# Order of the late expert teams, and the place of the first row fetch, in a routed-expert kernel on one core

## The chip, the core and the metric

The kernel runs on one core of a Trainium2 chip. The metric is the device time of one execution in microseconds (us). The core has a matrix engine (TensorE, "PE" in the profile), a vector engine (VectorE, "DVE"), a scalar engine (ScalarE, "ACT"), GpSimd ("POOL"), and SyncE ("SP"), which here only issues transfers. Sixteen DMA engines move data for all of them. An engine runs its own instructions in their order and waits on semaphores that the others raise.

## The reference

One block of three sublayers works on 256 tokens of width 512: cross-attention to 4096 memory rows under a mask, causal self-attention with 16 heads, and a layer of 64 experts of which each token takes 8. Only the last sublayer is touched:

```python
router_logits = x @ gate_w                                   # 256 x 64
routing_weights, selected = jax.lax.top_k(router_logits, K)  # K = 8
routing_weights = jax.nn.softmax(routing_weights, axis=-1)
hidden_sorted = jnp.repeat(x, K, axis=0)[order]              # rows sorted by expert
gate = jax.lax.ragged_dot(hidden_sorted, gate_proj_w, group_sizes)   # 512 -> 192 for each expert
up = jax.lax.ragged_dot(hidden_sorted, up_proj_w, group_sizes)
down = jax.lax.ragged_dot(jax.nn.silu(gate) * up, down_proj_w, group_sizes)
out = jnp.sum(down[unsort].reshape(-1, K, h) * routing_weights[..., None], axis=1)
```

The input x of this layer is layer-normed, and the result is added to the residual. An expert has 1152 KB of weights (gate 384, up 384, down 384), so the 64 experts have 72 MB, and each of them is read once whatever the routing is.

## The kernel before

**Teams and rounds.** The experts are worked off in 16 teams of four (`TEAM = 4`). TensorE takes a team in rounds of 32 rows for each of its four experts (`BLK = 32`), 128 rows in all, one quarter of the array's columns for each expert. So a team costs as many rounds as its largest expert has blocks of 32 rows, while its weights cost 4.5 MB of transfer however few rows it has.

**Order of the teams.** Teams 0, 1 and 2 (`EARLY = 3`) are experts 0 to 11 as numbered, so that their weights can be loaded before the routing is known. The other 52 experts are sorted by size on the chip (L819 to L822, `place` is the rank, largest first). The row `turn_row` says which rank stands at each position of the order: two iotas (L527 to L529) fill the pairs of teams, from `FIXED` upwards (the largest) and from `EXP_N - TEAM` downwards (the smallest), in turns, and a last one sets the middle team at the end. Counting the rows that the reference's router gives each expert for these inputs (0 to 138), the rounds of teams 0 to 15 are

```
3, 1, 1 | 5, 1, 3, 1, 3, 1, 2, 1, 2, 1, 1, 1, 1      28 rounds, numbered 0 to 27 below
```

**The ring.** Weights stand in a ring of four slots (`RING = 4`); team q uses slot q mod 4. SP issues 16 transfers for a team: gate and up of four experts (`load_gate_up`, L396), then down in two parts each (`load_down`, L403). Teams 0 to 2 are loaded during attention; team 3 once the list of teams is there (L417 to L418). From team 4 on (`reload`) SP first waits until TensorE has done the gate and up products (`s_gu`) of all rounds of the teams up to q - 4, issues the gate and up loads, waits for the same rounds' down products (`s_y`), and issues the down loads. `team_of` unpacks four expert numbers from one word into registers ahead of all issues (L385).

**A round on TensorE** (`one_round`, L1324): 32 gate and up products (L1329, `s_gu`); the mix of the last round's outputs into the tokens (L1251); products that turn the picks and give the weight of each slot (L1350, L1353, `s_mtp`); the turn of the hidden values (L1359); the turn of the next round's gathered rows (L1365), which waits until ACT has copied them (L1019); a product that gives the row numbers of the round three on (L1293); and 24 down products (L1378, `s_y`). Round 0 is written apart (`first=True`): rows for rounds 0 and 1 come from products with pick matrices (L1276), not from a gather, and before L1350 it waits for `s_wp` (weight parts, from POOL) and `s_tn`.

**Rows by gather.** From round 2 on POOL fetches a round's 128 rows (256 KB) of x from memory: `fetch(u, b)` is one small operation (L567) and an indirect transfer (L568) by the row numbers `row_no`, which DVE writes (L858, `s_idx`). In the loop POOL fetches round u, then waits for the landing of the fetch before it and says so (L625, `s_land`), and then forms rank differences for a later pick (L591, `differences`). ACT's copy L1019 waits for `s_land`. Ahead of the loop POOL does `differences(2)` and `differences(3)`, then four operations that split the router weights in three parts (L604 to L607, the last raises `s_wp`), then reads the number of rounds, then waits for the parts and the stored rows of x (`s_xp`, `s_xd`) and for `s_idx`, and issues the first fetch, `fetch(2, 0)`.

**Engines in a round.** DVE turns the slot weights from L1353 into `w_slot` (L884, L886); ACT scales the expert output with it (L1024); DVE finishes it (L890); the next round's L1251 takes both.

Of the kernel before, what the change touches and what calls it, by code (L numbers as in the profile page):

```python
# [19 lines left out]
P = 128  # L20
TOK, D = 256, 512
TH = TOK // P
# [7 lines left out]
EXP_N, TOPK, INTER = 64, 8, 192  # L30
TEAM = 4
# [5 lines left out]
FIXED = EARLY * TEAM  # L37
# [14 lines left out]
def perceiver(nc, x, ctxm, mask, w_qkv, w_out, q_gain, gate_w, gate_proj, up_proj, down_proj,  # L52
              rope_cs, out):
    es = ExitStack()
    with es:
# [7 lines left out]
        bank = [psum[:, i, :] for i in range(8)]  # L63
# [303 lines left out]
        def _(sp):  # L367
# [15 lines left out]
            def team_of(word):  # L383
                for j in range(TEAM):
                    sp.reg_mov(lanes[j], (word >> (6 * j)) & (EXP_N - 1))  # L385
                return [sp.snap(lanes[j], min_val=0, max_val=EXP_N - 1) for j in range(TEAM)]

            def word_of(q):
                return sp.value_load(team_word[0:1, bass.ds(q, 1)], min_val=0, max_val=EXP_N ** TEAM - 1)

            def load_gate_up(team, r):
                for j, e in enumerate(team):
                    lane = ring[r][:, j]
                    for dst, src in ((lane[:, 0:GU_W], gate_proj[bass.ds(e, 1)].rearrange("e (p c) n -> p (e c n)", c=DC)),
                                     (lane[:, GU_W:DOWN_AT], up_proj[bass.ds(e, 1)].rearrange("e (p c) n -> p (e c n)", c=DC))):
                        sp.dma_start(dst, src).then_inc(s_wg[r], 16)  # L396

            def load_down(team, r):
                for j, e in enumerate(team):
                    lane = ring[r][:, j]  # L400
                    for dst, src in ((lane[:, DOWN_AT:TAIL_AT], down_proj[bass.ds(e, 1), 0:MAIN_I].rearrange("e r n -> (e r) n")),
                                     (lane[:, TAIL_AT:SLOT_W], down_proj[bass.ds(e, 1), MAIN_I:].rearrange("e r (h n) -> (e r h) n", h=2))):
                        sp.dma_start(dst, src).then_inc(s_wd[r], 16)  # L403

            def load_team(team, r):
                load_gate_up(team, r)
                load_down(team, r)

            for r in range(EARLY - 1):
                load_team(range(r * TEAM, (r + 1) * TEAM), r)  # L410
# [15 lines left out]
            def reload(q, r):  # L426
                sp.reg_add(done, done, (sp.snap(left) & 7) + 1)
                sp.reg_mov(left, sp.snap(left) >> 3)
                team = team_of(word_of(q))
                sp.wait_ge(s_gu, sp.snap(done))  # L430
                load_gate_up(team, r)
                sp.wait_ge(s_y, sp.snap(done))
                load_down(team, r)
# [63 lines left out]
        def _(pool):  # L497
# [27 lines left out]
            pool.iota(turn_row[:, 0:FIXED], pattern=[[1, FIXED]], base=0, channel_multiplier=0,  # L525
                      allow_small_or_imprecise_dtypes=True).then_inc(s_tables, 1)
            pairs = turn_row[:, FIXED:EXP_N - TEAM].rearrange("p (m k j) -> p m k j", k=2, j=TEAM)  # L527
            for k, (base, stride) in enumerate(((FIXED, TEAM), (EXP_N - TEAM, -TEAM))):
                pool.iota(pairs[:, :, k], pattern=[[stride, LATE // 2], [1, TEAM]], base=base, channel_multiplier=0,  # L529
                          allow_small_or_imprecise_dtypes=True).then_inc(s_tables, 1)  # L530
            pool.iota(turn_row[:, EXP_N - TEAM:], pattern=[[1, TEAM]], base=FIXED + LATE // 2 * TEAM, channel_multiplier=0,
# [65 lines left out]
            differences(2)  # L597
            next_round()
            differences(3)

            part1 = w_rest
            zeros = zero[:, :].unsqueeze(2).to_broadcast([P, TH, EXP_N])
# [6 lines left out]
            n = pool.value_load(total[0:1, 0:1], min_val=TEAMS + 1, max_val=TEAMS * TOK // BLK)  # L609
            pairs = pool.alloc_register("pool_pairs")  # L610
            pool.reg_mov(pairs, n >> 1)
            pool.wait_ge(s_xp, 2)
            pool.wait_ge(s_xd, 32)
            pool.wait_ge(s_idx, 1)
            fetch(2, 0)
            next_round()
            differences(4)
            with pool.Fori(0, pool.snap(pairs, min_val=1, max_val=TEAMS * TOK // BLK)) as i:
# [421 lines left out]
        def _(pe):  # L1040
# [282 lines left out]
            def one_round(q, r, v, loads, first=False):  # L1323
                pe.wait_ge(s_xgc, v + 1)  # L1324
                for c in range(DC):
                    for e in range(TEAM):
                        quarter = slice(e * BLK, (e + 1) * BLK)
                        w = ring[r][:, e, 0:DOWN_AT].rearrange("p (g c n) -> p g c n", g=2, c=DC)
                        last = pe.matmul(bank[0][quarter, 0:2 * INTER], xs[:, c, quarter], w[:, :, c, :],  # L1329
                                         start=(c == 0), stop=(c == DC - 1))  # L1330
                last.then_inc(s_gu, 1)

                if first:
                    pe.wait_ge(s_pk, 3)
                    row_numbers(2)
                    pe.wait_ge(s_xgc, 1)
                    gather(picks[:, TOK:2 * TOK])

                if not first:
                    pe.wait_ge(s_yl, v)  # L1340
                    pe.wait_ge(s_mt, v)
                    mix(0)
                    mix(1)

                if first:
                    pe.wait_ge(s_wp, 1)
                    pe.wait_ge(s_tn, 1)
                slot = (v & (PICKS - 1)) * TOK
                for h in range(TH):
                    pe.matmul(bank[2][:, h * P:(h + 1) * P], picks[:, bass.ds(slot + h * P, P)], ident_b[:, :],  # L1350
                              start=True, stop=True)
                for h in range(TH):
                    last = pe.matmul(bank[2][:, TOK:TOK + 3 * TEAM], picks[:, bass.ds(slot + h * P, P)],  # L1353
                                     w_parts[:, h, :, q * TEAM:(q + 1) * TEAM], start=(h == 0), stop=(h == TH - 1))
                last.then_inc(s_mtp, 1)

                pe.wait_ge(s_h, v + 1)
                for k in range(2):
                    last = pe.transpose(bank[1][:, k * P:(k + 1) * P], hid[:, k * P:(k + 1) * P], ident[:, :])  # L1359
                last.then_inc(s_htp, 1)  # L1360

                if not first:
                    pe.wait_ge(s_row, v + 3)
                    for c in range(DC):
                        last = pe.transpose(bank[3][:, c * P:(c + 1) * P], x_rows[:, c::DC], ident[:, :])  # L1365
                    last.then_inc(s_xg, 1)
                pe.wait_ge(s_pk, v + 4)
                pe.wait_ge(s_idx, v + 1)
                row_numbers((v + 3) & (PICKS - 1))

                pe.wait_ge(s_wd[r], 16 * 2 * TEAM * loads)
                pe.wait_ge(s_ht, v + 1)
                for k, (cols, at) in enumerate(((slice(0, D), DOWN_AT), (slice(0, D // 2), TAIL_AT), (slice(D // 2, D), TAIL_AT))):
                    if k == 1:
                        pe.wait_ge(s_htt, v + 1)
                    for e in range(TEAM):
                        quarter = slice(e * BLK, (e + 1) * BLK)
                        last = pe.matmul(bank[6][quarter, cols], hidT[:, k, quarter],  # L1378
                                         ring[r][:, e, at:at + cols.stop - cols.start], start=(k == 0), stop=(k == 2))
                last.then_inc(s_y, 1)  # L1380

            pe.wait_ge(s_wg[0], 16 * 2 * TEAM)
            one_round(0, 0, 0, 1, first=True)
# [37 lines left out]
```

## Time and profile before

| what | us |
|---|---|
| median of 3 runs | 339.15 |
| the three runs | 339.88, 337.17, 339.15 |
| the profiled execution, its time | 338.92 |
| the profiled execution, its span | 337.2 |
| TensorE busy | 301.2 (89% of the span) |
| TensorE's weight loads busy | 170.2 (50%) |
| DVE busy | 165.6 (49%) |
| ACT busy | 100.6 (30%) |
| POOL busy | 76.0 (23%) |
| moved by DMA | 91.51 MB, mean 271 GB/s |

The span runs from the first to the last instruction of the profiled execution; 1.72 us of its time lie around it. "Busy" on PE is the time in which a matmul is in the pipeline, so it doesn't say how near PE is to its peak. "SPq", "POOLq" and "PEq" are the queues or sequencers of an engine: issuing, register and wait instructions. The expert layer begins at about 132 us of the span and takes the rest of it.

### The profile page before, as it was taken

Reading aid. Unit: us, or ns where it says so; the run is one execution under the profiler, and the core shown is the slowest. Engines: PE = TensorE matmul, PEld = TensorE weight load, DVE = VectorE, ACT = ScalarE, POOL = GpSimd, SP = SyncE. Lnnn points to the kernel's source line nnn. Section 1 sums busy time; section 2 is a strip of 40 time slices with the busy share of each in tenths; the row PEclk is TensorE's granted clock in tenths of the full one; section 3 lists DMA queues with packets and bytes.
Section 4 is the critical chain, followed back from the end, with each engine's and each line's share of the span. In section 5 each row is a group of like instructions: output and inputs, shape, how many; then the busy total and the mean of one; then the engine's idle time right before and its main releaser. Section 6 shows DMA issues by size and latency. Waiting matters only on the chain.

```text
span 337.2 us, 8802 instructions
## 1 busy us (share of the span) xinstructions
PE 301.2 (89%) x2667; PEld 170.2 (50%) x2667; DVE 165.6 (49%) x566; ACT 100.6 (30%) x196; POOL 76.0 (23%) x183
## 2 busy tenths in 40 slices
PE   0499999988999987869999999999999999999473
PEld 0363544444776444535555565555556555554231
DVE  7762285684397665424453444445344444534313
ACT  1120401115556153213332333333333233332212
POOL 5000001410000051632224223322422332232202
PEclk9999999999599999979999999999999999999969
DMA  2799996900000011975999969999999999999943
GB/s 68 284 398 398 386 391 191 385 14 3 0 2 2 13 49 39 342 266 179 391 394 386 394 197 363 389 392 393 387 394 390 387 398 387 390 396 384 387 152 95
DMA packets 42363, 91.51 MB, mean 271 GB/s; under 512 B 5144, under 2 KB 13472, under 8 KB 42208
## 3 DMA queue, kind: packets, MB, share of 16 engines
q1 hardware_dynamic: 39600, 83.51, 66.8%
q0 software_dynamic: 2320, 7.60, 6.3%
q8 instruction: 16, 0.26, 0.3%
q10 hardware_dynamic: 416, 0.04, 0.1%
q14 instruction: 11, 0.09, 0.1%
HBM read 90.09 MB, written 1.05 MB: 270 GB/s over the span
## 4 chain that ended last, share of the span: by engine, by line
PE 67%; DVE 9%; SPq 7%; issue 5%; ACT 4%; DMA 3%; POOL 2%; POOLq 1%; ACTq 0%; DVEq 0%
PE psum L1329 17%; PE psum L1378 13%; PE psum L1251 7%; PE psum L1069 4%; SPq L403 4%; PE psum L1108 4%; PE psum L1081 4%; DMA store<-in_L_ffn_up_proj_w_dram 3%; PE psum L1365 3%; PE psum L1169 2%; SPq L396 2%; PE psum L1359 2%; PE psum L1199 2%; PE psum L1060 2%; ACT store L959 2%
## 5 line engine op out<-in xcount | busy, mean ns | idle before, releaser
L1329 PE MATMUL psum<-store 128*32 128x384 f32 x896 | 79.8, 495 | 6.9 <-DMA store<-in_L_ffn_up_proj_w_dram 6.7
L1378 PE MATMUL psum<-store 128*32 128x256 f32 (+1 forms) x672 | 55.7, 464 | 0.4 <-DVE store L876 0.4
L1329 PEld LDWEIGHTS psum<-store 128*32 128x32 f32 x896 | 34.8, 112 | 40.6 <-issue 37.8
L890 DVE SCALAR_TENSOR_TENSOR y_parts<-psum,w_slot,y_parts 128x512 fp32r<-128x512 f32 x28 | 21.0, 751 | 58.4 <-ACT y_parts L1024 58.4
L1024 ACT ACTIVATE y_parts<-psum,w_slot 128x512 fp32r<-128x512 f32 x28 | 19.3, 688 | 57.9 <-PE psum L1378 57.9
L1251 PE MATMUL psum<-y_parts,place_T 128*128 128x512 f32 x112 | 33.8, 422 | 1.5 <-ACT y_parts L1024 1.4
L1378 PEld LDWEIGHTS psum<-store 128*32 128x32 f32 x672 | 23.0, 111 | 20.7 <-issue 9.5
L568 POOL DMA_INDIRECT store<-x_normed_rows,row_no x29 | 28.2, 974 | 13.1 <-issue 13.1
L1251 PEld LDWEIGHTS psum<-y_parts,place_T 128*128 128x128 f32 x112 | 18.8, 188 | 21.7 <-DVE y_parts L890 15.5
L567 POOL TENSOR_TENSOR ready<-zero 128x1 f32<-128x1 f32 x29 | 5.6, 194 | 103.8 <-DVE row_no L858 103.4
L1001 ACT ACTIVATE store<-psum 128x512 f32<-128x512 f32 x29 | 17.3, 598 | 33.5 <-PE psum L1365 31.4
L591 POOL TENSOR_TENSOR store<-store,slot_no 128x256 f32 x31 | 19.3, 622 | 22.5 <-issue 15.2
L871 DVE TENSOR_TENSOR store<-store,psum 128x128 f32<-128x128 f32 x28 | 8.1, 289 | 32.6 <-ACT store L1016 32.1
L1016 ACT ACTIVATE store<-psum 128x192 f32<-128x192 f32 x28 | 9.3, 332 | 44.5 <-PE psum L1329 44.5
L1108 PE MATMUL psum<-store,xnT 128*128 128x512 f32 x48 | 21.2, 594 | 0.8 <-ACT xnT L937 0.8
L1365 PE MATMUL psum<-ident,store 128*128 128x128 f32 x108 | 17.6, 286 | 3.1 <-ACT store L1019 3.1
L1019 ACT ACTIVATE store<-store 128x512 f32 x27 | 16.8, 623 | 3.5 <-POOL ready L625 3.5
L876 DVE COPY store<-psum 128x128 f32<-128x128 f32 x28 | 8.2, 292 | 19.6 <-PE psum L1359 19.6
L1365 PEld LDWEIGHTS psum<-ident,store 128*128 128x128 f32 x108 | 15.2, 209 | 3.3 <-ACT store L1019 3.3
L878 DVE TENSOR_SCALAR store<-psum,side 128x128 f32<-128x128 f32 x56 | 16.8, 342 | 0.0
L464 POOL TENSOR_TENSOR store<-store,cs_sb 128x128 f32<-128x128 f32 x8 | 3.4, 459 | 57.3 <-ACT store L940 57.3
L1069 PE MATMUL psum<-store,xnT 128*128 128x512 f32 x32 | 14.8, 605 | 0.0
(246 smaller groups left out, 396.6 us busy)
## 6 DMA issues: line engine op xcount, KB each, us to landing
store<-n_L_ffn_gate_proj_w_dram SPq DMA_DIRECT2D x64, 384.0 KB
store<-in_L_ffn_up_proj_w_dram SPq DMA_DIRECT2D x64, 384.0 KB
store<-n_L_ffn_down_proj_w_dram SPq DMA_DIRECT2D x64, 256.0 KB
store<-n_L_ffn_down_proj_w_dram SPq DMA_DIRECT2D x64, 128.0 KB
store<-in_L_attn_w_qkv_dram SPq DMA_DIRECT2D x1, 3072.0 KB, 15.2
store<-in_ctx_dram SPq DMA_DIRECT2D x2, 1024.0 KB, 6.7
store<-in_L_attn_w_out_dram SPq DMA_DIRECT2D x1, 1024.0 KB, 17.5
x_sb<-in_x_dram SPq DMA_DIRECT2D x1, 512.0 KB, 4.4
```

Of the source, the lines that this page charges most:

```text
L568: pool.indirect_dma_start(landing[:, b * D:(b + 1) * D], None, x_dram[:, :], bass.IndirectOffsetOnAxis(ap=row_no[:, b:b + 1], axis=0)).the ...
L591: pool.tensor_tensor(apart, ranks.unsqueeze(3).to_broadcast([P, TH, TEAM, BLK]), slot_no[:, bass.ds(r, 1), :].unsqueeze(1).to_broadcast([P ...
L878: last = dve.tensor_scalar(hidT[:, 1 + half], bank[1][:, P:2 * P], side[:, half:half + 1], None, ALU.mult)
L890: dve.scalar_tensor_tensor(y_parts[:, 1], bank[6], w_slot[:, :], y_parts[:, 0], ALU.mult, ALU.subtract).then_inc(s_yl, 1)
L1001: act.activation(xs, bank[3].rearrange("p (c s) -> p c s", c=DC), ACT.Copy).then_inc(s_xgc, 1)
L1024: act.activation(y_parts[:, 0], bank[6], ACT.Copy, scale=w_slot[:, :]).then_inc(s_yh, 1)
L1069: last = pe.matmul(b, xnT[:, c, h * P:(h + 1) * P], ctxT[:, j, c], start=False, stop=(c == DC - 1))
L1108: last = pe.matmul(bank[3 * h + j], xnT[:, c, h * P:(h + 1) * P], wqkv_sb[:, c, j * D:(j + 1) * D], start=(c == 0), stop=(c == DC - 1))
L1251: last = pe.matmul(bank[4 + h], place_T[:, h * P:(h + 1) * P], y_parts[:, part], start=False, stop=stop)
L1329: last = pe.matmul(bank[0][quarter, 0:2 * INTER], xs[:, c, quarter], w[:, :, c, :], start=(c == 0), stop=(c == DC - 1))
L1365: last = pe.transpose(bank[3][:, c * P:(c + 1) * P], x_rows[:, c::DC], ident[:, :])
L1378: last = pe.matmul(bank[6][quarter, cols], hidT[:, k, quarter], ring[r][:, e, at:at + cols.stop - cols.start], start=(k == 0), stop=(k == 2))
```

## The change

Three things are changed.

1. The two iotas of `turn_row` change places. The teams from 3 on are now the smallest, the largest, the second smallest, the second largest, and so on; the middle team stays last. By the same count as above the rounds of teams 0 to 15 are now `3, 1, 1 | 1, 5, 1, 3, 1, 3, 1, 2, 1, 2, 1, 1, 1`, again 28.
2. POOL waits for `s_xp`, `s_xd` and `s_idx` and issues `fetch(2, 0)` right after `differences(3)`, ahead of the four operations on the weights. On TensorE the slot weights of round 0 (L1353) and the waits for `s_wp` and `s_tn` move behind the round's down products.
3. For team 3 SP unpacks an expert's number just before it issues that expert's loads (`team_of` is a generator, and `load_team` passes on the list that `load_gate_up` has kept). `reload` still unpacks all four first.

```diff
             def team_of(word):
                 for j in range(TEAM):
                     sp.reg_mov(lanes[j], (word >> (6 * j)) & (EXP_N - 1))
-                return [sp.snap(lanes[j], min_val=0, max_val=EXP_N - 1) for j in range(TEAM)]
+                    yield sp.snap(lanes[j], min_val=0, max_val=EXP_N - 1)
...
             def load_gate_up(team, r):
+                loaded = []
                 for j, e in enumerate(team):
+                    loaded.append(e)
                     lane = ring[r][:, j]
...
+                return loaded
...
             def load_team(team, r):
-                load_gate_up(team, r)
-                load_down(team, r)
+                load_down(load_gate_up(team, r), r)
...
-                team = team_of(word_of(q))
+                team = list(team_of(word_of(q)))
...
-            for k, (base, stride) in enumerate(((FIXED, TEAM), (EXP_N - TEAM, -TEAM))):
+            for k, (base, stride) in enumerate(((EXP_N - TEAM, -TEAM), (FIXED, TEAM))):
...
             differences(3)
+            pool.wait_ge(s_xp, 2)
+            pool.wait_ge(s_xd, 32)
+            pool.wait_ge(s_idx, 1)
+            fetch(2, 0)
 
             part1 = w_rest
...
             pool.reg_mov(pairs, n >> 1)
-            pool.wait_ge(s_xp, 2)
-            pool.wait_ge(s_xd, 32)
-            pool.wait_ge(s_idx, 1)
-            fetch(2, 0)
             next_round()
...
-                if first:
-                    pe.wait_ge(s_wp, 1)
-                    pe.wait_ge(s_tn, 1)
                 slot = (v & (PICKS - 1)) * TOK
                 for h in range(TH):
                     pe.matmul(bank[2][:, h * P:(h + 1) * P], picks[:, bass.ds(slot + h * P, P)], ident_b[:, :],
                               start=True, stop=True)
-                for h in range(TH):
-                    last = pe.matmul(bank[2][:, TOK:TOK + 3 * TEAM], picks[:, bass.ds(slot + h * P, P)],
-                                     w_parts[:, h, :, q * TEAM:(q + 1) * TEAM], start=(h == 0), stop=(h == TH - 1))
-                last.then_inc(s_mtp, 1)
+
+                def slot_weights():
+                    for h in range(TH):
+                        last = pe.matmul(bank[2][:, TOK:TOK + 3 * TEAM], picks[:, bass.ds(slot + h * P, P)],
+                                         w_parts[:, h, :, q * TEAM:(q + 1) * TEAM], start=(h == 0), stop=(h == TH - 1))
+                    last.then_inc(s_mtp, 1)
+
+                if not first:
+                    slot_weights()
...
                 last.then_inc(s_y, 1)
+                if first:
+                    pe.wait_ge(s_wp, 1)
+                    pe.wait_ge(s_tn, 1)
+                    slot_weights()
```

## Rows read from the trace of the kernel before

**Rows 1.** Timeline, PE and its waits: start, duration, line, out<-in, count, [idle before <-releaser].

```profile
151.48 2.78 PE L1329 MATMUL psum<-store 128*32 128x384 f32 x32
...
302.01 2.79 PE L1329 MATMUL psum<-store 128*32 128x384 f32 x32
...
322.22 4.42 PE L1329 MATMUL psum<-store 128*32 128x384 f32 x32 [6.54 <-DMA store<-in_L_ffn_up_proj_w_dram]
```

**Rows 2.** Stretches: us, busy PE, PEld, DVE, ACT, POOL, PEclk, DMA share, GB/s.

```profile
150.00:155.00 5.00, 5.00 (x55) 2.31 (x45) 1.06 (x3) 1.36 (x3) 1.12 (x3) 0.85 0.16 56
...
196.00:203.00 7.00, 7.00 (x81) 3.93 (x77) 3.30 (x15) 2.36 (x5) 2.18 (x5) 1.00 0.54 162
203.00:228.00 25.00, 25.00 (x281) 14.39 (x274) 10.38 (x39) 7.95 (x15) 7.75 (x15) 1.00 1.03 380
228.00:322.00 94.00, 87.52 (x965) 49.51 (x964) 39.73 (x152) 29.05 (x54) 27.81 (x56) 0.98 1.04 390
```

**Rows 3.** Waits of SP's queue from 125 us on: total, times, longest.

```profile
SPq L396 <- PE psum L1329: 20.0, 4, 9.5
```

**Rows 4.** Timeline of SP: first issue for teams 4, 6, 7, 9 and 15.

```profile
154.47 0.33 SPq L396 DMA_DIRECT2D store<-n_L_ffn_gate_proj_w_dram  x1
...
178.99 0.34 SPq L396 DMA_DIRECT2D store<-n_L_ffn_gate_proj_w_dram  x1
...
200.28 0.33 SPq L396 DMA_DIRECT2D store<-n_L_ffn_gate_proj_w_dram  x1
...
226.47 0.33 SPq L396 DMA_DIRECT2D store<-n_L_ffn_gate_proj_w_dram  x1
...
306.90 0.34 SPq L396 DMA_DIRECT2D store<-n_L_ffn_gate_proj_w_dram  x1
```

**Rows 5.** Timeline of all engines, 135 to 149 us: rounds 0 and 1.

```profile
135.20 0.41 POOL L604 TENSOR_TENSOR store<-store,zero 128x128 bf16<-128x128 f32 x1
...
135.67 0.14 DVE L858 CAST row_no<-psum 128x1 int32<-128x1 f32 x1
...
136.67 0.43 POOL L607 TENSOR_TENSOR store<-store 128x128 bf16<-128x128 f32 x1
...
137.16 0.28 PE L1350 MATMUL psum<-ident_b,store 128*128 128x128 bf16 x2 [0.59 <-POOL store L607]
...
137.49 0.19 POOL L567 TENSOR_TENSOR ready<-zero 128x1 f32<-128x1 f32 x1 [0.39 <-issue]
...
138.23 1.93 PE L1378 MATMUL psum<-store 128*32 128x512 f32 x24 [0.45 <-DVE store L876]
138.26 1.14 POOL L568 DMA_INDIRECT store<-x_normed_rows,row_no  x1 [0.58 <-issue]
...
139.95 2.79 PE L1329 MATMUL psum<-store 128*32 128x384 f32 x32
...
146.27 0.20 POOL L625 TENSOR_TENSOR ready<-zero 128x1 f32<-128x1 f32 x1 [4.66 <-DMA store<-x_normed_rows,row_no]
...
147.35 0.75 PE L1365 MATMUL psum<-ident,store 128*128 128x128 f32 x4 [3.05 <-ACT store L1019]
...
148.10 3.58 PE L1378 MATMUL psum<-store 128*32 128x512 f32 x24
```

**Rows 6.** Stretches with a lowered clock (columns as in rows 2).

```profile
83.30:84.40 1.10, 1.10 (x5) 0.43 (x3) 0.00 (x0) 1.10 (x4) 0.00 (x0) 0.50 0.05 15
...
147.30:151.40 4.10, 4.05 (x30) 2.04 (x34) 0.93 (x5) 0.60 (x2) 2.60 (x5) 0.60 0.58 209
...
322.20:326.70 4.50, 4.48 (x33) 1.48 (x34) 0.00 (x0) 0.00 (x0) 0.00 (x0) 0.62 0.36 127
```

**Rows 7.** Fetch for round 4: timeline of its issue; DMA view, 150.8 to 152.5: packets, MB.

```profile
149.33 0.97 POOL L568 DMA_INDIRECT store<-x_normed_rows,row_no  x1 [0.45 <-issue]
...
q0 software_dynamic: 80, 0.26, 44.4%
```

**Rows 8.** SP's register instructions in `team_of`: ns min, median, max.

```profile
L385 SPq FUSED_REGOPS  x52: 3/64/409, 132.1 to 306.6; - x52
```

## The prediction, as it stood before the run

> **What bounds the kernel now.** I read the profile in this order: the timeline of TensorE over the expert layer, the stretches of DMA traffic, SP's waits and issues, then the two first rounds instruction by instruction. The reader should see two resources taking turns. From round 2 on TensorE has no idle time: L1329 starts at 151.48 for round 2 and at 302.01 for round 25, so a round takes (302.01 - 151.48) / 23 = 6.545 us [rows 1]. The last round, 27, would then start at 302.01 + 2 x 6.545 = 315.1 us. It starts at 322.22, after 6.54 us of waiting for the last gate and up weights [rows 1]. So the end is set by DMA. DMA works at 390 GB/s in 228 to 322 us, its full share, but not all of the time: it moves 56 GB/s in 150 to 155, 162 in 196 to 203, 380 in 203 to 228 [rows 2]. At 390 that is lost time of 4.3, 4.1 and 0.6 us. The losses have their cause in SP, which waits 20.0 us in four times for L1329 [rows 3], that is for a slot of the ring. The two that cost: team 4 is first issued at 154.47, just behind round 2's L1329 (151.48 + 2.78 = 154.26), since slot 0 is free only then; team 7 at 200.28, behind round 9, the last of the five rounds of team 3, the largest [rows 1, 4]. From there SP and DMA never catch up, and a team costs DMA (306.90 - 226.47) / 6 = 13.4 us against 6.5 us for a team of one round on TensorE [rows 4].
>
> **The order of the teams.** It removes no work: 28 rounds and 13 late teams in both. What moves is which rounds free a slot. I write G(r) for the end of round r's L1329, which by rows 1 is 154.26 + 6.545 (r - 2) as the kernel is. Before, team 7 needs G(9) = 200.1. After, team 3 has one round, so team 7 needs only G(5) = 173.9, while SP would come to it one step of 13.4 after team 6 at 178.99, at 192.4 [rows 4]: no wait. The five rounds are now team 4's, rounds 6 to 10, and team 8 in the same slot needs G(10) = 206.6. SP would come to it at 192.4 + 13.4 = 205.8; with 3 to 4 us of weights still queued then (the issue of a team's last transfers runs ahead of the traffic), 0.8 us late costs DMA nothing. The later ones by the same sum: team 10 needs G(14) = 232.8 and is due at 206.6 + 26.8 = 233.4; team 12 needs G(18) = 259.0, due 260.2; team 14 needs G(21) = 278.6, due 287.0. So DMA runs through. The gain is the loss around 200 us: 4.1 + 0.6 = 4.7 us by bandwidth [rows 2]; by issues, nine steps from team 6 to team 15 take 306.90 - 178.99 = 127.9 instead of 9 x 13.4 = 120.6, which gives 7.3 [rows 4]. I take 5.0, near the bandwidth, because an issue time says how far SP is ahead as well. The cap is TensorE: with round 27 bound to 315.1 no more than 7.1 can come.
>
> Does TensorE now wait for weights earlier? Team 4 is needed at round 6 (L1329 at 151.48 + 4 x 6.545 = 177.7), before at round 10. The last team's gate and up weights land at most 322.22 - 306.90 = 15.3 us after its first issue [rows 1, 4]; for team 4 that is 169.8, 8 us ahead. Later teams have more: team 13 (round 25) starts 24 us after it is there.
>
> **The fetch.** POOL's chain L604 to L607 runs from 135.20 to 136.67 + 0.43 = 137.10; reading the count and the waits make L567 start at 137.49 and L568 at 138.26, 0.77 later [rows 5]. After the change L567 can start when the row numbers are written (L858 ends at 135.81, so about 135.95), and L568 at about 136.65 to 136.7: 1.6 us earlier. TensorE's wait is 3.05 us at L1365 in round 1, at the end of a chain of fetch, L625 and ACT's copy [rows 5]. Behind it L1378 takes 3.58 us instead of 1.93: clock 0.60 of full in 147.3 to 151.4, part of it at the 1.2 GHz level, after TensorE had been idle [rows 5, 6]. That is another 1.65. So the stall costs 4.7 in all, from which slot 0's release follows one for one, and with it team 4's issue and, DMA now running through, everything to the end. (As the kernel is, it would also be one for one: the 5-round team's release moves too.)
>
> How much of it goes? Issue to L625 was 146.27 - 138.26 = 8.0 us beside the loads of team 3 [rows 5]. Bound below, same latency: L1365 moves from 147.35 to 145.75. Bound above, the latency of a fetch without other traffic: that for round 4 is issued at 149.33 and its packets, 0.26 MB, all lie in 150.8 to 152.5, so about 3 us [rows 7]; then the stall is gone, since POOL's next fetch ends before TensorE is ready. I take a latency half a microsecond under the loaded one (less of team 3 is queued at 136.7 than at 138.3): L1365 at 145.3, 2.05 us earlier. The stall left is about 1 us, and I expect the clock to stay up: +1.65, together 3.7. The case against stands in rows 6: in 83.3 to 84.4 the clock is at half behind gaps of about 1 us, so a short stall can cost some clock too. The range for this part is 1.6 to 4.6.
>
> The Trainium skill ("DMA: Bandwidth & Descriptors", section on the anatomy of one DMA on the gpsimd path) fits such a transfer by 2.0 us plus bytes at 436 GB/s, 2.6 us for 256 KB. The trace agrees for the unloaded fetch (about 3) and not for the loaded one (8.0). By the page alone the stall would vanish, and the part would be 4.5 instead of 3.7.
>
> **What the fetch displaces.** L604 to L607 and `s_wp` come behind L567 and L568: L568 ends at about 137.8, the chain of 1.9 us at 139.8 instead of 137.1. TensorE no longer waits for it at L1350 (0.59 us idle there [rows 5]), so the turn of the hidden values and L1378 come 0.4 earlier, 137.85 to 139.8. Then the slot weights wait till 139.8, two small products of 0.2 us, and round 1's L1329 starts at about 140.2 against 139.95. These 0.25 us fall into the stall that is left, so they cost nothing; if the stall is gone, they count, and I have them in the 4.6 (4.7 less some). The weights reach DVE, ACT's L1024 and L890 0.7 to 1.4 us later, but are needed only behind L1329 of round 1, at 143.0. The next fetch followed the first one's L568 (end 138.26 + 1.14 = 139.40 [rows 5]) by one `differences`; now it follows the chain's end at 139.8, the read of the count and one `differences`, so by my estimate it goes out 0.9 later, at about 141.5. With the same 8.0 us it has landed at 149.5, and ACT wants it after G(2), then 150.6. That is 1 us of cover; if gone, it costs one for one.
>
> **SP.** `team_of` has one register operation of median 64 ns [rows 8] and a shorter one for each expert; three of the four experts move behind the first issue, about 0.5 us. Team 3 is needed at round 5, 20 us after its weights are there, so this is worth nothing.
>
> **The last rounds.** The start of L1329 in round 27 moves from 322.22 by 3.7 + 5.0 to 313.5. TensorE is bound to 315.1 - 3.7 = 311.4, so its wait shrinks from 6.54 to about 2 us, and the clock need not fall: L1329 at 4.42 in a stretch of clock 0.62 becomes 2.79 [rows 1, 6]. That is 1.6 more.
>
> **Sum.** 3.7 + 5.0 + 1.6 = 10.3 us. Against its own profiled execution, span 337.2 becomes 326.9 and time 338.92 becomes 328.6. That execution lies 0.2 under the median of 339.15, so the median should become 328.8.
>
> **The rivals.** (A) The fetch lands without a stall: 4.6 instead of 3.7, and TensorE rather than DMA may set round 27; 327.9. (B) The reorder works and the fetch brings nothing, because its latency grows by what it is early (it only waits longer behind team 3's packets), or the wait for the slot weights takes its place: 5.0 + 1.6 = 6.6, so 332.5. For it speaks that a loaded fetch waits in the DMA engines, against it that nothing queues ahead of it that was not there before. With half of that, or with clock lost at a short stall, 330.5. (C) The reorder brings nothing: DMA drains once more, now before team 8, as it is bound to G(10). The fetch alone gives 3.7, so 335.4. It decides if the queue is empty at 203; by the sum above 3 us are left. (D) Slower than before: team 4, five rounds early, starves TensorE at round 6 and everything shifts one for one. It starts to count when its gate and up weights land after 177.7 - 3.7 = 174.0, 23 us after their issue at 150.8 instead of 15.3, and it turns the result only above 33 us; nothing in the rows takes so long.
>
> **Chances.** Forecast, with the half cases up to 330.5: 0.65. A: 0.12. B: 0.14. C: 0.06. D: 0.03. The range goes from 326.0 (A, and a gain of 6.5 instead of 5.0 by the reorder) to 332.6 (B). About 1% (3.4 us) is what a measurement of this kernel can tell from no change; its three runs lie 2.7 us apart. Faster by over 1% (under 335.8) holds forecast, A, B and half of C: 0.94, less for D's neighbours 0.93; same 0.04; slower 0.03.
>
> **What would show it.** Order: SP's first issue of team 7 at about 189 and of team 8 at about 203, no stretch under 350 GB/s between 160 and 310, the last L1329 at 313.5 with a wait of about 2 us. Fetch: L568 first at 136.7, L1365 of round 1 at 145.3 with under 1.5 us idle, L1378 behind it at 1.9 and not 3.6, team 4 issued at about 150.8. Displaced: round 1's L1329 at 140.2, no idle at round 2's L1365. It is wrong if DMA has a hole before team 8, if the clock falls in round 1, or if round 27 still waits over 4 us.

## The result: 10 us faster, and the profile after

| what | before | changed |
|---|---|---|
| median, us | 338.16 (4 runs, 335.79 to 339.88) | 328.11 (4 runs, 325.62 to 330.79) |
| ratio, 95% interval | | 0.968 (0.959 to 0.978) |
| profiled execution, span | 337.2 | 326.0 |
| TensorE busy | 301.2 | 297.7 |

The two medians lie 10.05 us apart, the two profiled spans 11.2. The forecast was 328.8, from a sum of 10.3. (The median of before, 338.16, has one execution more than the 339.15 that the forecast started from.) How much of this belongs to the change, and how much to where the clock happened to fall, is a question of its own that the experiments answer below. Medians here and below are of all executions of a kernel; ratios and their intervals are of its fast ones alone, those at most 1.5% above its fastest, so the two need not agree.

First the traffic in the changed kernel: stretches, with the columns of [rows 2].

```profile
150.00:155.00 5.00, 5.00 (x57) 3.16 (x61) 2.45 (x11) 2.13 (x4) 2.25 (x5) 1.00 0.75 237
...
196.00:203.00 7.00, 7.00 (x75) 4.13 (x74) 3.15 (x13) 2.59 (x6) 1.98 (x4) 1.00 1.03 395
203.00:228.00 25.00, 25.00 (x284) 14.34 (x285) 11.27 (x44) 7.90 (x15) 7.92 (x16) 1.00 1.04 392
228.00:310.00 82.00, 82.00 (x900) 47.07 (x896) 36.39 (x141) 27.05 (x51) 23.94 (x49) 1.00 1.04 390
```

The hole of [rows 2] in 196 to 203, 162 GB/s, is gone; DMA runs at 390 to 395 through to 310 us, and in steps of 20 us no stretch from 160 to 310 is under 388. The first hole, before team 4, is still there but shorter: in steps of 2 us, 175 and 101 GB/s from 148 to 152, where before has 246, 133, 6 and 78 from 148 to 156. SP's waits for L1331 (the old L1329) fell from 20.0 us in four times [rows 3] to 7.4 in three, of which 6.0 are before team 4:

```profile
SPq L398 <- PE psum L1331: 7.4, 3, 6.0
```

SP's first issues of teams 4, 7, 8 and 15, from the timeline, answer to [rows 4]:

```profile
150.14 0.33 SPq L398 DMA_DIRECT2D store<-n_L_ffn_gate_proj_w_dram  x1
...
188.04 0.33 SPq L398 DMA_DIRECT2D store<-n_L_ffn_gate_proj_w_dram  x1
...
202.51 0.33 SPq L398 DMA_DIRECT2D store<-n_L_ffn_gate_proj_w_dram  x1
...
297.60 0.34 SPq L398 DMA_DIRECT2D store<-n_L_ffn_gate_proj_w_dram  x1
```

Team 7 comes 12 us earlier than before, and from team 4 to team 15 SP needs 147.5 us instead of 152.4. Rounds 0 to 2 and the last round, from the timeline of all engines, answer to [rows 5] and [rows 1]:

```profile
135.56 0.19 POOL L569 TENSOR_TENSOR ready<-zero 128x1 f32<-128x1 f32 x1 [0.57 <-DVE row_no L860]
...
136.33 1.13 POOL L570 DMA_INDIRECT store<-x_normed_rows,row_no  x1 [0.58 <-issue]
...
140.01 2.79 PE L1331 MATMUL psum<-store 128*32 128x384 f32 x32 [0.34 <-issue]
...
141.25 0.62 POOL L593 TENSOR_TENSOR store<-store,slot_no 128x256 f32 x1 [1.85 <-issue]
...
142.11 0.29 DVE L855 TENSOR_SCALAR store<-store 128x256 f32 x1 [1.70 <-POOL store L593]
...
143.12 1.19 PE L1253 MATMUL psum<-y_parts,place_T 128*128 128x512 f32 x4 [0.32 <-DVE y_parts L892]
...
143.61 0.19 POOL L627 TENSOR_TENSOR ready<-zero 128x1 f32<-128x1 f32 x1 [0.36 <-DMA store<-x_normed_rows,row_no]
...
144.69 0.75 PE L1369 MATMUL psum<-ident,store 128*128 128x128 f32 x4
...
145.43 1.93 PE L1382 MATMUL psum<-store 128*32 128x512 f32 x24
...
147.15 2.79 PE L1331 MATMUL psum<-store 128*32 128x384 f32 x32
...
313.26 2.79 PE L1331 MATMUL psum<-store 128*32 128x384 f32 x32 [2.24 <-DMA store<-in_L_ffn_up_proj_w_dram]
```

The fetch goes out at 136.33, its landing is told at 143.61, and the row of L1369 (the old L1365) shows no wait; L1382 (the old L1378) takes 1.93, not 3.58. The last round waits 2.24 instead of 6.54 us and its L1331 takes 2.79 instead of 4.42. There is one new wait, 0.32 us of L1253 (the old L1251), to which I come back below. The span differs by 11.2 us: 0.24 before round 0 (L1331 at 132.03 instead of L1329 at 132.27), 4.09 up to round 2 (147.15 against 151.48, less the 0.24), 4.63 more up to the last L1331 (313.26 against 322.22), 1.63 in its duration, and 0.6 behind it, on which more at the end.

### The profile page after: what moved, and what is told of

Same layout as the page of the kernel before. It is cut to its first block, busy times and chain, and to the rows that moved or that the text cites. A ratio compares the mean times of both kernels' runs of the same rounds, so it can differ in the third digit from the quotient of the medians.

```text
span 326.0 us, 8801 instructions
## 1 busy us (share of the span) xinstructions
PE 297.7 (91%) x2667; PEld 169.3 (52%) x2667; DVE 165.4 (51%) x566; ACT 100.5 (31%) x196; POOL 75.8 (23%) x183
## 4 chain that ended last, share of the span: by engine, by line
PE 52%; SPq 19%; DVE 10%; issue 6%; ACT 4%; DMA 4%; POOL 2%; POOLq 1%; DVEq 0%; ACTq 0%
PE psum L1331 11%; SPq L406 11%; PE psum L1382 8%; SPq L398 6%; PE psum L1253 5%; PE psum L1071 4%; PE psum L1110 4%; PE psum L1083 4%; DMA store<-in_L_ffn_up_proj_w_dram 4%; PE psum L1369 2%; PE psum L1171 2%; PE psum L1201 2%; ACT store L961 2%; PE psum L1155 1%; PE psum L1363 1%
## 5 line engine op out<-in xcount | busy, mean ns | idle before, releaser
L1331 PE MATMUL psum<-store 128*32 128x384 f32 x896 | 78.1, 486 | 2.8 <-DMA store<-in_L_ffn_up_proj_w_dram 2.2
L1382 PE MATMUL psum<-store 128*32 128x256 f32 (+1 forms) x672 | 54.0, 453 | 0.4 <-DVE store L878 0.4
L1331 PEld LDWEIGHTS psum<-store 128*32 128x32 f32 x896 | 34.5, 110 | 34.4 <-issue 31.5
L892 DVE SCALAR_TENSOR_TENSOR y_parts<-psum,w_slot,y_parts 128x512 fp32r<-128x512 f32 x28 | 21.0, 750 | 39.5 <-ACT y_parts L1026 39.5
L1253 PE MATMUL psum<-y_parts,place_T 128*128 128x512 f32 x112 | 33.8, 422 | 1.2 <-ACT y_parts L1026 0.8
L1382 PEld LDWEIGHTS psum<-store 128*32 128x32 f32 x672 | 22.7, 109 | 19.7 <-issue 8.2
L1253 PEld LDWEIGHTS psum<-y_parts,place_T 128*128 128x128 f32 x112 | 18.8, 188 | 21.5 <-issue 16.2
L593 POOL TENSOR_TENSOR store<-store,slot_no 128x256 f32 x31 | 19.2, 620 | 25.6 <-issue 18.3
L1369 PE MATMUL psum<-ident,store 128*128 128x128 f32 x108 | 17.7, 286 | 0.0
L1021 ACT ACTIVATE store<-store 128x512 f32 x27 | 16.8, 623 | 0.8 <-POOL ready L627 0.8
L1369 PEld LDWEIGHTS psum<-ident,store 128*128 128x128 f32 x108 | 15.2, 209 | 0.2 <-ACT store L1021 0.2
```

The costliest lines, as they stand in the source:

```text
L593: pool.tensor_tensor(apart, ranks.unsqueeze(3).to_broadcast([P, TH, TEAM, BLK]), slot_no[:, bass.ds(r, 1), :].unsqueeze(1).to_broadcast([P ...
L892: dve.scalar_tensor_tensor(y_parts[:, 1], bank[6], w_slot[:, :], y_parts[:, 0], ALU.mult, ALU.subtract).then_inc(s_yl, 1)
L1253: last = pe.matmul(bank[4 + h], place_T[:, h * P:(h + 1) * P], y_parts[:, part], start=False, stop=stop)
```

## Experiments

Line numbers move by a few between the kernels: the gate and up products are L1329, L1331, L1333 or L1335, and the turn of the gathered rows in round 1 is L1365, L1367 or L1369.

**The order alone.**

```diff
-            for k, (base, stride) in enumerate(((FIXED, TEAM), (EXP_N - TEAM, -TEAM))):
+            for k, (base, stride) in enumerate(((EXP_N - TEAM, -TEAM), (FIXED, TEAM))):
```

> The kernel before with the two iotas exchanged and nothing else. Theory 1 (two independent parts): the stall of round 1 stays (about 3.0 us idle, then a lowered clock), team 4 is first issued at 154.5 as before, but the hole in the traffic at 196 to 203 us is gone; the last L1329 starts at about 316.7 instead of 322.2, waits under 2 us and takes 2.8 instead of 4.4; span about 329.7, time 7.5 us under before. Theory 2 (the parts need each other, since without the earlier fetch the five-round team frees its slot too late): a hole before team 8 at about 205 to 208 us, the last L1329 at 319 or later, time 2 to 4 us under before.

Median 331.48 us (10 executions, 327.25 to 335.19) against 337.80 of before on the same chip: 6.3 less where 7.5 was expected, ratio 0.977 (0.969 to 0.985). Its timelines of TensorE and of SP have the stall and no hole:

```profile
142.08 0.75 PE L1365 MATMUL psum<-ident,store 128*128 128x128 f32 x4 [2.35 <-ACT store L1019]
142.85 3.15 PE L1378 MATMUL psum<-store 128*32 128x512 f32 x24
...
149.24 0.33 SPq L396 DMA_DIRECT2D store<-n_L_ffn_gate_proj_w_dram  x1
...
297.66 0.00 SPq L396 DMA_DIRECT2D store<-n_L_ffn_gate_proj_w_dram  x1
...
312.66 2.79 PE L1329 MATMUL psum<-store 128*32 128x384 f32 x32 [2.52 <-DMA store<-in_L_ffn_up_proj_w_dram]
```

Team 4 to team 15 take 148.4 us, 4.0 less than before, without the early fetch. So the order does not need the fetch. But the span was 326.0 where 329.7 was expected, and everything in it lies about 4 us earlier than it should. Round 0 already starts at 127.72 instead of 132.27, in code that the edit does not touch. That was the first sign of the clock's part, below.

**The fetch, the slot weights and SP's part, in the old order.** Edit: the changed kernel with the line above turned back.

> The changed kernel with the old order of the teams (early fetch, moved slot weights and SP's unpacking stay). Theory 1: round 2's L1331 starts at 147.2 as in the changed kernel, 4.1 us of stall and lowered clock gone; the hole before team 7 is there again, 4.1 us earlier; the last L1331 waits about 6.5 us and takes 4.4; span about 333.0, time 4.2 under before. Theory 2 (the hole before team 7 takes up what the fetch gives): time equal to before within 1 us.

Median 335.88 (10 executions, 332.56 to 339.03): 1.9 less than before by the medians, ratio 0.999 (0.994 to 1.005). That rules out the 4.2 us of theory 1; the ratio is what theory 2 expected, the medians lie between the two. The stall was nearly gone (L1369 waited 0.29), SP waited 16.7 us again, and the last L1331 waited 6.42 and took 5.03. The executions of one kernel lay 6 us apart, so that a part of 2 us could not be told from none. Whether the hole takes up what the fetch gives is decided further down.

**SP's unpacking, and the place of the slot weights.** Edits: the changed kernel with

```diff
-                    yield sp.snap(lanes[j], min_val=0, max_val=EXP_N - 1)
+                return [sp.snap(lanes[j], min_val=0, max_val=EXP_N - 1) for j in range(TEAM)]
```

> The changed kernel, but SP unpacks all four experts of team 3 ahead of its first issue, as before. My theory: worth nothing; first issue for team 3 about 0.5 us later (132.5), everything from round 0 on within 0.3 us of the changed kernel, span 326. Rival: the earlier start of team 3 is what let the traffic reach team 4 without a hole and the fetch land in time; then round 1's L1369 waits and the time is 1 to 2 us over the changed kernel.

and, in another kernel, with TensorE's slot weights of round 0 and their two waits back at their old place.

> The changed kernel, but TensorE waits for the weight parts and makes the slot weights of round 0 ahead of the turn of the hidden values, as before. My theory: the weight parts come at 139.4, so the turn starts at about 139.8 instead of 136.7, round 1's L1331 at about 142.6 instead of 140.0, and from there all is 2 to 2.8 us late: span about 328.5; most of what the earlier fetch gave is lost. Rival: the loss lies inside the wait for the gathered rows and costs nothing; span 326.

The first gave 330.21 (4 executions, 327.16 to 332.56), the second 331.68 (327.33 to 334.15). In the first the landing came 0.75 later after round 0's start than in the changed kernel and L1369 waited 0.63; the time lies in the range that the rival named, 2.1 over the changed kernel, but the two were measured apart and their ranges overlap. So it stayed undecided and was taken up again below. In the second the wait is plain:

```profile
142.21 0.28 PE L1352 MATMUL psum<-ident_b,store 128*128 128x128 bf16 x2 [2.88 <-POOL store L613]
```

TensorE stands 2.88 us for the weight parts that now come behind the fetch. In this execution the clock was lowered in round 0 as well (its first L1331 took 4.62 us), so the loss is not sized; the median is 3.6 over the changed kernel, which was measured apart, and 1.5 over the first of these two beside it, with ranges that overlap. That TensorE stands for the weight parts when the slot weights stay where they were is shown; what it costs in time is not.

**What makes the executions differ.** The stretches around the start of self-attention, before, then in the kernel with the order alone (columns as above):

```profile
84.00:95.00 11.00, 11.00 (x91) 8.05 (x90) 5.25 (x9) 5.04 (x12) 0.00 (x0) 0.57 0.01 1
```

```profile
84.00:95.00 11.00, 10.82 (x162) 8.36 (x162) 9.06 (x17) 9.00 (x22) 0.00 (x0) 1.00 0.01 3
```

It is the same code. In the profile of before the granted clock is mostly at the 1.2 GHz level here, behind a wait of 1.08 us of TensorE at 81.3 to 82.3; in the other it stays at 2.4, and round 0 starts 4.5 us earlier. The same wait stands in all six profiles so far; four of them show the fall (before, the changed kernel with 0.60, SP as before, the slot weights as before) and two do not. So a short wait sometimes costs the clock and sometimes does not, and the profiles of before and of the changed kernel, compared above, both have the fall. To measure the parts without this, I filled that wait in all four combinations:

```diff
             pe.wait_ge(s_qkd, 2)
+            for _ in range(5):
+                pe.matmul(bank[1], later_b[:, 0, 0:P], later_b.rearrange("p h t -> p (h t)"), start=True, stop=True)
             for g in range(HG):
```

> The changed kernel with five matmuls whose result nobody reads (1.1 us) in the wait of about 1.1 us that TensorE has at the start of self-attention. Theory: that wait is where the clock sometimes falls to half for 10 us; with it filled the clock stays up, round 0's L1331 starts at 127.7 us (as in the runs where it did not fall) instead of 132.0, the rest is as in the changed kernel (194.0 us from there), span 321.7, time 323.4, and the executions lie closer together than 5 us. Rival: the filler only delays self-attention by 1 us and the clock falls as often: span 327, spread as before.

> The kernel before with the same five matmuls. Base for the two next ones. Theory: round 0's L1329 at 127.7, from there 204.9 us as in the profile of before: span 332.6, time 334.3, and before minus changed, both filled, is 10.9 us. Rival (part of the 11 us was luck with the clock outside the expert layer): the difference is under 9 us.

> The kernel before with the iotas exchanged, and the five matmuls. Theory 1 (parts independent): the order alone gives 6.6 us against the filled kernel before (5.0 at the last L1329's start, 1.6 of its duration): time 327.7, stall of 2.4 to 3.1 us in round 1. Theory 2 (the order needs the fetch): under 4 us.

> The changed kernel with the old order of teams, and the five matmuls. Theory 1: 4 us against the filled kernel before: time 330.2, no stall over 0.7 us in round 1, hole in the traffic before team 7, the last L1331 waits 6.5 us and takes 4.4 to 5. Theory 2 (what the fetch gives is taken up by the hole): under 1.5 us.

| with the filler | median, us | 4 executions, us | span of the profile |
|---|---|---|---|
| before | 333.33 | 332.76 to 334.21 | 332.5 |
| order alone | 327.45 | 326.20 to 328.22 | 325.8 |
| fetch, slot weights, SP | 331.70 | 330.99 to 333.16 | 331.5 |
| all of the change | 325.95 | 324.55 to 326.56 | 322.8 |

The unfilled kernel before ran at 338.60 beside them (337.97 to 339.28). The changed kernel was expected at a span of 321.7 and a time of 323.4: the profile came within 1.1 us, the median 2.5 over it. All four profiles have the clock at full in 84 to 95 us, and the executions of each kernel lie 1.5 to 2.2 us apart. (The unfilled kernel before lay only 1.3 apart beside them, so a smaller spread is not shown; that the filler brings this kernel from 338.60 to 333.33 is.) Now the parts can be told: the order gives 5.9 us without the fetch and 5.75 with it; the fetch gives 1.6 without the order and 1.5 with it. By my estimate from the spread of four executions each of these differences can be off by 1.5, so the order's part is clear and each of the fetch's is only just clear of nothing. The fastest executions say the same: 6.6 and 6.4 for the order, 1.8 and 1.65 for the fetch. The parts are independent, as theory 1 said, and rival C (order brings nothing) is out. The size of the fetch's part, though, was expected at 4 by theory 1 and under 1.5 by theory 2; what rules theory 2 out is that the fetch gives no more in the new order, where there is no hole to take it up. Together the parts give 7.4 us, not the 10.9 expected here: the rival of that expectation (part of the 11 us was luck with the clock) is what came out.

The profiles say where the rest is. In the filled kernel before, the clock fell elsewhere:

```profile
123.00:134.00 11.00, 10.14 (x68) 6.43 (x72) 4.18 (x21) 3.06 (x5) 2.22 (x5) 0.53 0.39 131
```

It fell over the routing part and round 0. That is not this kernel's alone: with the filler in the attention wait, four of six profiles show it in this stretch, at 0.53 here and 0.84 in the three others. Of the table, both kernels in the old order have it in their profile and both in the new order have not; how the executions without a profile stand is not known, so a part of the order's 5.9 could be this. Against that, the unfilled profiles of before and of the changed kernel have it in neither, and give 4.63 + 1.63 = 6.3 for the order. Here it made round 0 start 2 us and end 4 us later than in the kernel with the order alone, while team 3's loads did not wait for it at all and the fetch went out only 2.1 later. So the gather was nearly there when TensorE asked: L1367 waited 0.29 us, against 2.41 in the profile of the filled kernel with the order alone. A stall in one place and a lowered clock ahead of it hide each other. In the one pair of profiles that has no lowered clock ahead of round 1 (order alone and all of the change, both filled) the fetch is worth what was forecast in kind: team 4 is first issued at 146.39 instead of 149.33, the last team at 294.02 instead of 296.98, the span is 322.8 instead of 325.8. That is 3.0 us. The medians of the same two kernels differ by 1.5; the other executions of the full change show a lower mean clock than the profiled one (0.990 to 0.992 against 0.998), and in which stretch they lost it no profile shows.

**The ring, pushed both ways.** With the filled changed kernel, all late teams from smallest to largest (the edit shown), and from largest to smallest (the same with `[[TEAM, LATE], [1, TEAM]]` and `base=FIXED`):

```diff
-            pairs = turn_row[:, FIXED:EXP_N - TEAM].rearrange("p (m k j) -> p m k j", k=2, j=TEAM)
...
+            pool.iota(turn_row[:, FIXED:], pattern=[[-TEAM, LATE], [1, TEAM]], base=EXP_N - TEAM, channel_multiplier=0,
+                      allow_small_or_imprecise_dtypes=True).then_inc(s_tables, 3)
```

> The changed kernel with the attention filler and the late teams from smallest to largest (rounds 3, 1, 1 | 1 eight times, 2, 2, 3, 3, 5). Theory (a team costs DMA 13.4 us and TensorE 6.545 us a round, in a ring of four slots): from team 6 on TensorE waits about 6.9 us for each team of one round, traffic has no hole, and the five rounds of the last team run with nothing left to load; the last L1333 starts 38.5 us later than in the changed kernel, span about 361. This is the starvation of the slower rival, made to happen. Rival: TensorE's waits are filled some other way, since total work is the same; span under 340.

> The same with the late teams from largest to smallest (rounds 3, 1, 1 | 5, 3, 3, 2, 2, 1 eight times). Theory: slots come free too slowly, so SP waits and the traffic has holes before teams 7, 8 and 9 (first issues at about 192, 212 and 231 us when round 0 starts at 127.7), then TensorE waits 5.6 to 6.9 us for each of the last three teams; the last L1333 starts 18 us later than in the changed kernel and runs at a lowered clock; span about 343. Rival: under 333.

Smallest first: span 358.0, time 359.75. TensorE's waits (sum in us, times, longest):

```profile
PE psum L1329 <- DMA store<-in_L_ffn_up_proj_w_dram: 22.8, 6, 4.7
```

and in its timeline the last L1329, which starts 35.8 us later than in the filled changed kernel:

```profile
345.29 2.79 PE L1329 MATMUL psum<-store 128*32 128x384 f32 x32
```

Largest first: span 340.8, time 342.54. SP waits 39.1 us in six times, and the first issues of teams 7, 8 and 9 are

```profile
193.77 0.33 SPq L398 DMA_DIRECT2D store<-n_L_ffn_gate_proj_w_dram  x1
...
213.41 0.33 SPq L398 DMA_DIRECT2D store<-n_L_ffn_gate_proj_w_dram  x1
...
233.05 0.33 SPq L398 DMA_DIRECT2D store<-n_L_ffn_gate_proj_w_dram  x1
```

against 192, 212 and 231 expected for a round 0 at 127.7 (it started at 129.26). The same sum of 13.4 us a team and 6.545 us a round that made the forecast gives both spans within 3 us (361 and 343 expected), in one execution of each. The waits of TensorE in the first were 22.8 us and not 41: behind each wait the clock was lowered (the L1329 behind the six waits took 4.17 to 5.35 us instead of 2.79), and slower rounds took the place of waiting, at no cost as DMA was the bound at 389 to 392 GB/s from 160 to 228. So starvation by small teams, the mechanism of rival D, is real. It came here with eight one-round teams in a row; in the alternating order only the last round waits.

**A faster kernel, and SP once more.** The filler, and idle matmuls in two waits of the routing part:

```diff
+            keep_clock(0, 5)
             pe.wait_ge(s_rw, 1)
             flip(0)
+            keep_clock(0, 2)
             pe.wait_ge(s_trn, 1)
```

> The changed kernel with the attention filler and, as a candidate for a faster kernel, five and two more idle matmuls in the two waits of the routing part (1.45 and 0.7 us before L1271 and L1285). Theory: some executions of the kernels with the first filler still lose 1.6 us or more to a lowered clock at 123 to 134 us, because TensorE is busy only 3.8 of 6 us there; with the waits filled it stays up, median 324.5 with less spread. Rival: the fillers delay the chain to the teams' list, which is on the path; median 326.5 or more.

> The same as the kernel before it, but SP unpacks all four experts ahead of team 3's first issue. My theory: worth nothing, within 0.7 us of the kernel before it. Rival (the earlier start of team 3's loads lets the first fetch land earlier): 1 us or more slower.

Medians 324.39 (324.00 to 329.26) and 324.49 (323.20 to 326.40), ratio of the first to before 0.966 (0.950 to 0.982). SP's unpacking makes 0.1 us between the medians. Four executions each can miss 2 us, so it is the profiles that speak against the rival: without SP's edit the fetch landed 12.17 us after round 0's start, with it 12.49. The one execution in which it landed later, above, was not more than what varies. The kernel filled twice is the fastest in its median, 3.7 us under the changed one. The two never ran side by side, the single filler's ratio to before, 0.9635 (0.9613 to 0.9657), is as good, and one execution in four still was at 329.26. For the kernel before it is shown that filling the attention wait helps (338.60 and 333.33 side by side); for the changed one it is 2.2 us between medians measured apart, and that the second filler adds to it is not shown.

## Why the prediction was right, and where its terms were off

**What bounds the kernel**: right. The last round waited for weights and the ring starved DMA; the order alone took the hole away.

**The order of the teams**: 5.0 forecast at the last round's start. Measured 4.6 in the profile after, 5.0 by its issues, 4.0 by the issues with the order alone. With the 1.6 us of the last L1329, 6.6 forecast; 5.9 by the filled medians. Team 7 was due at about 189 and came at 188.04, team 8 at 203 and came at 202.51. The bound of 4.7 by bandwidth was met. The 7.3 by issues was too high, since it took a step of 13.4 us for all: nine steps from team 6 to team 15 took 297.60 - 174.66 = 122.9 us in the changed kernel, not 120.6. The 3 to 4 us of weights still queued when team 8 comes had no row behind them, but the cover was there: SP waited 1.4 us in all for slots after team 4's, and the traffic shows no hole at 203. One margin was read wrong without effect: team 13's weights were not 24 us early. By the prediction's own sums they are due at 273.6 + 15.3 = 288.9 and used at 302.0, which is 13, and the margin shrinks with each team up to the last, which is late.

**The fetch**: right in kind, and the term that was mis-sized. The step was "Issue to L625 was 8.0 us ... I take a latency half a microsecond under the loaded one". It was 143.61 - 136.33 = 7.3 in the profile after, and 7.0 to 8.1 in the others in which POOL stood waiting for it; so the loaded latency held. The fit of the Trainium skill ("DMA: Bandwidth & Descriptors", section on the anatomy of one DMA on the gpsimd path) gives 2.6 us for it, which did not hold beside the loads here. The wait that I left at 1 us was 0 to 0.8 on the row of the turn. The profile pair gave 4.1 (3.7 forecast), the filled pairs 1.6 and 1.5 in the median, near the half case of rival B. What failed is that I took the 4.7 of stall and lowered clock as present in every execution, and 3.7 of it as regained. In the filled kernel before, with the clock lowered ahead of round 1, the stall was 0.29 us and there was next to nothing to remove. That a rest of the stall lowers the clock again, the risk that I had named, shows in none of the profiles: behind waits of 0.2 to 0.8 us the down products of round 1 took 1.93.

**What the fetch displaces**: round 1's gate and up products were forecast at 140.2 and started at 140.01. That the slot weights had to move with it is argued from the 2.88 us of the kernel without. One wait was overlooked: the prediction has the weights "needed only behind L1329 of round 1, at 143.0", and reckons only with their arrival. But L892 (the old L890), which works on their product, stands on DVE behind L855, and that waits 1.70 us for POOL's L593, now behind the weight parts. So L1253 waits 0.32 us. It cost nothing here, as forecast for a different reason: L1369 started at 144.69, and ACT's copy L1021 ended only at 144.64, so the wait lies in what is left of the stall. That rest is 0.6 us, for round 1 lasted 147.15 - 140.01 = 7.14 us instead of 6.545. The second fetch was forecast at 141.5 and was issued at 142.26, since POOL stood 1.85 us ahead of `differences(4)`; its landing was told at 148.98, 1.0 us before ACT's silu of round 2 at 150.00. The cover held, by as little as forecast.

**SP's unpacking**: 0 forecast, 0.1 measured, within what can be told.

**The last rounds**: forecast start 313.5, wait 2 us, duration 2.8; measured 313.26, 2.24, 2.79. The duration is not safe, though. In seven other profiles of the new order the last wait was 1.4 to 2.5 us, and in one of them, the one filled twice with SP as before, the clock fell behind it all the same, which cost the 1.6 us again:

```profile
310.31 4.43 PE L1335 MATMUL psum<-store 128*32 128x384 f32 x32 [2.38 <-DMA store<-in_L_ffn_up_proj_w_dram]
```

**The sum**: 10.3 forecast, 10.05 measured. It agreed better than its terms deserve, and that is in part luck. With the attention wait filled the change is worth 7.4. The rest goes with the clock: the unfilled kernel before loses 5.3 us beside its filled form (338.60 and 333.33), the changed one about 2.2 (328.11 and 325.95, measured apart). Why the changed one should lose less is not shown. My sum took the clock places of one profiled execution of before as given, and that happened to be near the usual case.

## What to carry to other kernels

In a ring of buffers that is filled at a constant rate and drained at a rate that varies by item, write down for each refill when its slot comes free and when the queue would get to it; put a short item ahead of the longest, so that the refill which waits for the longest item's slot comes one turn later, when the queue only just gets to it, and check the other end, where several short items in a row starve the consumer. When an instruction is moved ahead of others on a slow engine, move the consumers of what it displaces too. Where executions of one kernel differ by more than the effect, look for a stretch whose clock differs between their profiles, fill the wait before it in both kernels, and compare those.

## What the runs showed of the hardware that I had not expected

- A wait of TensorE of 1.08 us was followed by some 10 us at a lowered clock in some executions and by none in others of the same code, 0.57 against 1.00 of full clock in 84 to 95 us, and 4.5 us of time at round 0. It fell in four of six profiles; with five idle matmuls (1.25 us together) in the wait it fell in none of eight.
- In 123 to 134 us the clock was lowered in two of the six profiles without a filler and in four of the six with the one filler (0.53 once, else 0.82 to 0.84 of full), and in neither of the two with the waits of the routing part filled too.
- A gather of 256 KB took 7.0 to 8.1 us from its issue to the notice of its landing beside a full load, and about 3 us without [rows 7].
- In the last round ACT's scaling started 1.98 to 1.99 us after the first of the 24 down products in the changed kernel and in four more profiles (smallest first, largest first and the two filled twice), and 2.57 to 2.60 us after it in the nine others (before, the four unfilled experiments, and the four of the table). It is 0.6 us at the end of the kernel, goes with neither part of the change, and stays open.
